# Rounded halves for seven of the last product's projections in a six-product graph kernel

## The chip, the cores and the metric

One core of a Trainium2 chip runs the kernel. The metric is the device time of one execution in microseconds (us), as a median over runs. Engines are named as in the profile: PE is TensorE's matmul, PEld its load of stationary values, DVE is VectorE, ACT is ScalarE, POOL is GpSimd, SP is SyncE.

## The reference, cut to what matters

Everything is fp32. `adj` is a sparse 4096x4096 matrix stored densely, `x` is 4096x128.

```python
def mlp(x, W1, b1, W2, b2, W3, b3):        # leaky_relu with slope 0.01 after each
    x = a(x @ W1 + b1); x = a(x @ W2 + b2)
    return a(x @ W3 + b3)

u = x
for _ in range(3):                          # the third u is not used
    v = mlp(adj @ u, uv_W1, ..., uv_b3)
    u = mlp(adj @ v, vu_W1, ..., vu_b3)
x = layernorm(x + v)                        # products 0 to 4 of the kernel
x = layernorm(x + adj @ (x @ weight))       # product 5: computed as (adj @ x) @ weight
```

## The kernel before, in words

There are six products `adj @ p`, five with the layers of an `mlp` behind them (the fifth with a layer norm too), and a last one, product 5, with one projection by `gcn_W` and a layer norm. The matrix is read as tiles of 256 columns by 512 rows of `adj` (128 x 1024 fp32 in SBUF). Each product has eight output chunks of 512 rows, and each chunk is a sum over 16 tiles in one PSUM bank of 512 columns.

**Halves.** A factor of a product is not used as fp32. ACT rounds it to fp32r (`high`, `p_high`, `h_high`) and DVE subtracts that from the value (`low`, `p_low`, `h_low`), and PE then adds three passes: low by high, high by high, high by low. For the matrix this is done for each tile: SP loads it into one of eight `raw` places, two tiles at a time, ACT writes `high` (L446), DVE writes `low` (L570), both in rings of eight slots. For the stationary side it is done once for each chunk of the vector `p`; `p_high[i]` and `p_low[i]` are 128x4096 each, with i the parity of the product, so product 5 reads the set 1 and product 4 the set 0.

**Order.** All engines walk over the same list of steps. Step n of PE is visit n: one tile times its two stationary blocks, six matmuls of 512 columns (`multiply`, L790). There are 768 visits of 500 tiles, since some tiles serve two products while they are in SBUF. The last product begins in step 594 and is alone from step 686 on. ACT rounds a tile up to 6 steps (`AHEAD`) before PE first visits it, DVE subtracts 4 steps before. Each engine's queue is in order, so whatever is put into step n on an engine stands ahead of the tile work of that step.

**The work of a chunk of the last product** (`not layered(i)`, chunks 40 to 47 of 48) is placed relative to its `start`, the step in which its sum is complete. The starts are 710, 713, 722, 725, 736, 739, 752 and 768.
- start: DVE adds the sum in PSUM and the part kept in SBUF into `h[i % 2]` (`finish`, L604, total_ready). For the last chunk ACT copies the sum instead (`take`).
- start + 4 (`PROJECT`): PE projects, `project` with `turning`: four blocks of `h` are the stationary side, `gcn_W` moves with 128 columns, both fp32, into the one bank `proj`. It waits until the chunk before has been added (x_added), as that empties `proj`.
- start + 5: DVE `measure`: adds the residual (L640), takes statistics (L644, L647). It waits for normed_ready of the chunk before.
- start + 6 and + 7: ACT `deviation` (L504); DVE `invert` (L654, L656, `shift`).
- start + 8: ACT `normalize`, four instructions (L513), and a store from POOL, for the last two chunks from SP.

The layers of the other products run with halves too where `chunk.halves` is set (`dense`, L708 to L711), all but the third, which is an fp32 projection by `turning`.

Of the kernel before, what the change touches and what calls it, by code (L numbers as in the profile page):

```python
# [12 lines left out]
D = 128  # L13
# [34 lines left out]

THIRD, P_LOWER = 1, 2
MEASURE, ROOT, INVERT, NORMALIZE, NORM_P_LOWER = 2, 3, 4, 5, 6  # L50

PROJECT, LAST_MEASURE, LAST_ROOT, LAST_INVERT, LAST_NORMALIZE = 4, 5, 6, 7, 8

# [193 lines left out]
def gnn_kernel(nc, adj, x_nodes, weights, biases, spread, out):  # L247
# [4 lines left out]
    with ExitStack() as ctx:  # L252
# [6 lines left out]
        def sem(name):  # L259
            return ctx.enter_context(nc.semaphore(name))  # L260
# [41 lines left out]
        sum_raised = sem("sum_raised")  # L302
        sum_lowered = sem("sum_lowered")
        taken = sem("taken")
        layer_1_done = sem("layer_1_done")
        first_raised = sem("first_raised")
        first_ready = sem("first_ready")
# [58 lines left out]

        def layered(i):
            return i < FINAL

        def plain(i):  # L370
            return i < NORM
# [69 lines left out]
        def _(act):  # L441
# [75 lines left out]
            def raise_normed(i):  # L517
                c = sum_of(i).chunk
                act.wait_ge(normed_ready, i - NORM + 1)
                act.wait_ge(visited, over_with(LAST - 2, c))  # L520
                nc.scalar.activation(p_high[LAST % 2][:, blocks_of(c)], resid[:, blocks_of(c)],
                                     ACT.Copy).then_inc(p_high_ready, 1)

            def take(i):
                wait_sum(i)
                if plain(i - 2):
                    act.wait_ge(p_low_ready, CHUNKS + i - 1)
                nc.scalar.activation(h[i % 2][:], acc[sum_of(i).bank][:], ACT.Copy).then_inc(taken, 1)

            for n in range(END):  # L530
                if n == TILES - 1:
                    raise_weights()
                for i, chunk in enumerate(chunks):
                    if n == chunk.start and not chunk.halves and not finishes(i):
                        take(i)
                    if layered(i):
                        if n == chunk.start and chunk.halves:
                            raise_sum(i)
                        if n == chunk.start + (LAYER_1 if chunk.halves else WHOLE_LAYER_1):
                            first_layer(i)  # L540
                        if n == chunk.start + (LAYER_2 if chunk.halves else WHOLE_LAYER_2):
                            second_layer(i)
                        if n == chunk.third + THIRD:
                            third_layer(i)
                    if normed(i):
                        if n == chunk.third + ROOT:
                            deviation(i)
                        if n == chunk.third + NORMALIZE:
                            normalize(i)
                            raise_normed(i)  # L550
                    if not layered(i):
                        if n == chunk.start + LAST_ROOT:
                            deviation(i)
                        if n == chunk.start + LAST_NORMALIZE:
                            normalize(i)
                for s in sums:
                    if s.goal == "keep" and n == s.read:
                        keep(s)
                for t in range(len(tiles)):
                    if n == split_at[t]:  # L560
                        if t % IN_BAND == 0 and t // IN_BAND < CHUNKS:
                            raise_x(t // IN_BAND)
                        split(t)
# [3 lines left out]
        def _(dve):  # L567
# [91 lines left out]
            def lower_normed(i):  # L659
                c = sum_of(i).chunk  # L660
                dve.wait_ge(p_high_ready, CHUNKS + i + 1)
                nc.vector.tensor_tensor(p_low[LAST % 2][:, blocks_of(c)], resid[:, blocks_of(c)],
                                        p_high[LAST % 2][:, blocks_of(c)].bitcast(F32),
                                        ALU.subtract).then_inc(p_low_ready, 1)

            for n in range(END):
                if n == TILES - 1:
                    lower_weights()
                for i, chunk in enumerate(chunks):
                    if n == chunk.start and finishes(i):  # L670
                        finish(i)
                    if layered(i):
                        if n == chunk.start + LOWER_SUM and chunk.halves:
                            lower_sum(i)
                        if n == chunk.start + LOWER_FIRST and chunk.halves:
                            lower_first(i)
                        if n == chunk.third:
                            add_bias(i)
                    if plain(i) and n == chunk.third + P_LOWER:
                        lower_third(i)  # L680
                    if normed(i):
                        if n == chunk.third + MEASURE:
                            measure(i)
                        if n == chunk.third + INVERT:
                            invert(i)
                        if n == chunk.third + NORM_P_LOWER:
                            lower_normed(i)
                    if not layered(i):
                        if n == chunk.start + LAST_MEASURE:
                            measure(i)  # L690
                        if n == chunk.start + LAST_INVERT:
                            invert(i)
                for s in sums:
                    if s.goal == "more" and n == s.read:
                        grow(s)
                for t in range(len(tiles)):
                    if n == lowered_at[t]:
                        if t % IN_BAND == 0 and t // IN_BAND < CHUNKS:
                            lower_x(t // IN_BAND)
                        split(t)  # L700
# [3 lines left out]
        def _(pe):  # L704
# [8 lines left out]
            def wait_sum(i):  # L713
                if finishes(i):
                    pe.wait_ge(total_ready, sum_of(i).nth + 1)
                else:
                    pe.wait_ge(taken, unsummed(i) + 1)
# [25 lines left out]
            def turning(i, source, weight):  # L743

                for j in range(IN_CHUNK):
                    done = nc.tensor.matmul(block_in(proj, j), block_in(source, j), weight[:], start=True,  # L746
                                            stop=True)
                done.then_inc(proj_done, 1)
# [5 lines left out]
                turning(i, h[i % 2], w[f"{way_of(i)}_W3"])  # L754

            def project(i):
                wait_sum(i)
                if i > FINAL:
                    pe.wait_ge(x_added, i - NORM)
                else:  # L760
                    pe.wait_ge(biased, FINAL)
                turning(i, h[i % 2], w["gcn_W"])

            def wait_bank(before):
# [76 lines left out]
```

## Time and profile before

| | |
|---|---|
| time, median of 3 runs | 1181.62 us (1181.33 to 1182.02) |
| the profiled execution | 1181.15 us, of which the profile's span is 1179.2 us |
| PE busy | 1154.8 us, 98% |
| DVE busy | 739.8 us, 63% |
| ACT busy | 680.8 us, 58% |
| mean granted clock of PE | 0.999 of full speed |
| last product alone | from about 1048 us to the end |

A start in a timeline is in us from the beginning of the span. The recorded duration of a matmul contains its latency: neighbouring starts tell its cost. An instruction of DVE or ACT can start a little before the end of the one ahead of it. Idle time in brackets names what released the instruction. One fp32 matmul leaves two records of a load and a matmul, one of fp32r leaves one.

### The profile page before, as it was taken

The page shows a single profiled execution, that of the slowest core. Times are in us where ns is not written, and L with a number is a line of the kernel's source. Part 1 is how long each engine was busy: PE and PEld are TensorE (multiplying, and loading weights), DVE is VectorE, ACT ScalarE, POOL GpSimd, SP SyncE. Part 2 cuts the span into 40 slices and gives each one's busy share as a digit, 9 for nine tenths or more (in the row PEclk, how much of TensorE's full clock was granted, in tenths as well). Part 3 has the DMA queues.
Part 4 walks back from the last instruction along what each step waited for, and adds up shares of the span by engine and source line. Part 5 has one row for each costly group of instructions (what it writes and reads, how often), then busy time and mean ns, then how long its engine had stood idle before and what let it go on. Part 6 is the DMA issues. An engine that isn't in the chain of part 4 may idle for free.

```text
span 1179.2 us, 13786 instructions
## 1 busy us (share of the span) xinstructions
PE 1154.8 (98%) x5216; PEld 950.7 (81%) x5216; DVE 739.8 (63%) x879; ACT 680.8 (58%) x855; POOL 10.5 (1%) x24
## 2 busy tenths in 40 slices
PE   5999999999999999999999999999999999999997
PEld 3788888888788888888888878888887888888886
DVE  5986555554845554765564484555578655669996
ACT  5876544555554444764454474544477655557784
POOL 2000000000000000000000000000000000000000
PEclk9999999999999999999999999999999999999999
DMA  8987665644834446645544574444657454458994
GB/s 351 382 317 276 230 248 214 250 160 189 306 148 186 178 185 219 261 169 193 214 183 162 209 289 176 178 178 178 250 215 266 162 185 181 185 195 342 353 347 173
DMA packets 37823, 267.82 MB, mean 227 GB/s; under 512 B 4464, under 2 KB 4464, under 8 KB 5632
## 3 DMA queue, kind: packets, MB, share of 16 engines
q1 hardware_dynamic: 36864, 264.78, 60.0%
q0 software_dynamic: 896, 2.17, 0.5%
q8 instruction: 43, 0.70, 0.2%
q14 instruction: 20, 0.16, 0.0%
HBM read 264.83 MB, written 2.10 MB: 226 GB/s over the span
## 4 chain that ended last, share of the span: by engine, by line
PE 91%; DVE 5%; DMA 3%; ACT 1%; issue 1%; ACTq 0%; SPq 0%; DVEq 0%
PE acc L790 82%; PE proj L746 3%; DVE low L570 3%; DMA raw<-adj_dram 3%; PE layer L711 1%; PE layer L708 1%; PE layer L709 1%; PE layer L740 1%; PE layer L729 1%; DVE stats L644 0%; ACT part L513 0%; DVE h L640 0%; ACT high L446 0%; DVE h L604 0%; DVE moments L647 0%
## 5 line engine op out<-in xcount | busy, mean ns | idle before, releaser
L790 PE MATMUL acc<-high,p_low 128*128 128x512 f32 x1536 | 609.3, 397 | 14.2 <-DVE low L570 14.2
L570 DVE TENSOR_TENSOR low<-raw,high 128x1024 fp32r<-128x1024 f32 x500 | 584.5, 1218 | 36.8 <-ACT high L446 36.8
L790 PE MATMUL acc<-low,p_high 128*128 128x512 f32 x1536 | 599.6, 390 | 0.0
L790 PE MATMUL acc<-high,p_high 128*128 128x512 f32 x1536 | 598.9, 390 | 0.0
L446 ACT ACTIVATE high<-raw 128x1024 fp32r<-128x1024 f32 x500 | 500.2, 1050 | 80.9 <-DMA raw<-adj_dram 40.8
L790 PEld LDWEIGHTS acc<-high,p_low 128*128 128x128 f32 x1536 | 289.1, 188 | 78.9 <-DVE low L570 17.8
L790 PEld LDWEIGHTS acc<-high,p_high 128*128 128x128 f32 x1536 | 289.1, 188 | 61.4 <-issue 2.9
L790 PEld LDWEIGHTS acc<-low,p_high 128*128 128x128 f32 x1536 | 288.9, 188 | 61.4
L473 ACT ACTIVATE h_high<-h 128x512 fp32r<-128x512 f32 x21 | 13.3, 632 | 134.1 <-DVE h L604 134.1
L604 DVE TENSOR_TENSOR h<-acc,part 128x512 f32<-128x512 f32 x36 | 24.8, 689 | 100.8 <-PE acc L790 93.2
L614 DVE TENSOR_TENSOR h_low<-h,h_high 128x512 fp32r<-128x512 f32 x32 | 22.1, 692 | 70.2 <-ACT h L483 70.2
L619 DVE TENSOR_TENSOR h<-proj,b_uv_b 128x512 f32<-128x512 f32 x24 | 16.6, 690 | 63.9 <-PE proj L746 63.9
L609 DVE TENSOR_TENSOR h_low<-acc,h_high 128x512 fp32r<-128x512 f32 x11 | 7.6, 691 | 77.8 <-ACT h_high L473 77.8
L498 ACT ACTIVATE p_high<-h 128x512 fp32r<-128x512 f32 x32 | 20.2, 632 | 48.5 <-DVE h L619 48.0
L473 ACT ACTIVATE h_high<-acc 128x512 fp32r<-128x512 f32 x11 | 6.6, 596 | 72.1 <-PE acc L790 72.1
L619 DVE TENSOR_TENSOR h<-proj,b_vu_b 128x512 f32<-128x512 f32 x16 | 11.1, 691 | 41.6 <-PE proj L746 41.6
L488 ACT ACTIVATE h<-layer,b_uv_b 128x512 f32<-128x512 f32 x24 | 16.5, 688 | 30.3 <-PE layer L711 24.3
L481 ACT ACTIVATE h_high<-layer,b_uv_b 128x512 fp32r<-128x512 f32 x20 | 13.7, 686 | 34.1 <-PE layer L711 34.1
L500 ACT ACTIVATE h<-h 128x512 f32<-128x512 f32 x40 | 24.8, 620 | 9.9 <-DVE h L619 9.8
L746 PEld LDWEIGHTS proj<-w_uv_W,h 128*128 128x128 f32 x192 | 25.1, 191 | 2.0
L463 ACT ACTIVATE part<-acc 128x512 f32<-128x512 f32 x36 | 21.4, 595 | 7.4 <-PE acc L790 7.0
L746 PE MATMUL proj<-w_uv_W,h 128*128 128x128 f32 x192 | 25.3, 275 | 0.0
(64 smaller groups left out, 379.6 us busy)
## 6 DMA issues: line engine op xcount, KB each, us to landing
raw<-adj_dram SPq DMA_DIRECT2D x250, 1024.0 KB, 4.9
out_dram<-part POOLq DMA_DIRECT2D x6, 256.0 KB, 5.1
resid<-x_dram SPq DMA_DIRECT2D x1, 1024.0 KB, 18.2
resid<-x_dram SPq DMA_DIRECT2D x2, 256.0 KB, 5.9
resid<-x_dram SPq DMA_DIRECT2D x1, 512.0 KB, 13.0
out_dram<-part SPq DMA_DIRECT2D x2, 256.0 KB, 2.0
w_uv_W<-uv_W_dram POOLq DMA_DIRECT2D x3, 64.0 KB, 7.8
w_vu_W<-vu_W_dram POOLq DMA_DIRECT2D x3, 64.0 KB, 7.9
```

What stands on the lines that cost most here:

```text
L446: nc.scalar.activation(high[t % SLOTS][:], raw_of(t), ACT.Copy).then_inc(high_ready, 1)
L463: nc.scalar.activation(part_of(s.chunk), acc[s.bank][:], ACT.Copy).then_inc(part_kept, 1)
L473: nc.scalar.activation(h_high[:], summed(i)[:], ACT.Copy).then_inc(sum_raised, 1)
L488: nc.scalar.activation(h[i % 2][:], layer[1][:], ACT.Prelu, bias=b[f"{way_of(i)}_b2"][:], alpha=SLOPE).then_inc(second_ready, 1)
L498: nc.scalar.activation(p_high[k % 2][:, blocks_of(c)], h[i % 2][:], ACT.Prelu, alpha=SLOPE).then_inc(p_high_ready, 1)
L500: nc.scalar.activation(h[i % 2][:], h[i % 2][:], ACT.Prelu, alpha=SLOPE).then_inc(third_ready, 1)
L570: nc.vector.tensor_tensor(low[t % SLOTS][:], raw_of(t), high[t % SLOTS][:].bitcast(F32), ALU.subtract).then_inc(low_ready, 1)
L604: nc.vector.tensor_tensor(h[i % 2][:], acc[s.bank][:], part_of(s.chunk), ALU.add).then_inc(total_ready, 1)
L614: nc.vector.tensor_tensor(h_low[:], h[i % 2][:], h_high[:].bitcast(F32), ALU.subtract).then_inc(first_lowered, 1)
L619: nc.vector.tensor_tensor(h[i % 2][:].rearrange("p (j d) -> p j d", d=D), proj[:].rearrange("p (j d) -> p j d", d=D), b_spread[f"{way_of(i ...
L746: done = nc.tensor.matmul(block_in(proj, j), block_in(source, j), weight[:], start=True, stop=True)
L790: done = nc.tensor.matmul(bank[:], p[parity][:, at:at + D], a[slot][:, columns], start=(n == s.opens and j == 0 and m == 0), stop=(n == s. ...
```

## The change

Seven of the eight chunks of the last product (`projects_halves(i)`: chunks 40 to 46) are projected in three passes of rounded halves. The room for them is the stationary set 0, which product 4 no longer reads from step 686 on: `spare_of(i)` are the first seven blocks of 512 columns of `p_high[0]` and `p_low[0]`, and `SPARE_W` the first 128 columns of the eighth, for `gcn_W`. Added are:
- once: ACT rounds `gcn_W` in step 707 (`raise_gcn`), DVE subtracts in step 708 (`lower_gcn`), 128x128 each.
- for each of the seven chunks: ACT rounds `h` (128x512) in step start, ahead of the other work of that step (`raise_last`); it waits for total_ready. DVE subtracts in step start + 1 (`lower_last`).
- on PE, in place of four fp32 matmuls (128x128 by 128x128): twelve fp32r matmuls of the same shape, behind waits for `last_lowered` and `gcn_lowered` in place of total_ready.

Chunk 47 is projected as before. Nothing changes in the order of the visits, the loads from HBM or the buffers of the tiles.

```diff
--- before.py
+++ after.py
@@ -48,6 +48,7 @@
 
 THIRD, P_LOWER = 1, 2
 MEASURE, ROOT, INVERT, NORMALIZE, NORM_P_LOWER = 2, 3, 4, 5, 6
+
 
 PROJECT, LAST_MEASURE, LAST_ROOT, LAST_INVERT, LAST_NORMALIZE = 4, 5, 6, 7, 8
 
@@ -302,6 +303,10 @@
         sum_raised = sem("sum_raised")
         sum_lowered = sem("sum_lowered")
         taken = sem("taken")
+        gcn_raised = sem("gcn_raised")
+        gcn_lowered = sem("gcn_lowered")
+        last_raised = sem("last_raised")
+        last_lowered = sem("last_lowered")
         layer_1_done = sem("layer_1_done")
         first_raised = sem("first_raised")
         first_ready = sem("first_ready")
@@ -367,6 +372,16 @@
         def layered(i):
             return i < FINAL
 
+        def projects_halves(i):
+            return FINAL <= i < len(chunks) - 1
+
+        def spare_of(i):
+            return blocks_of(i - FINAL)
+
+        SPARE_W = bass.ds((CHUNKS - 1) * CHUNK, D)
+
+        FREED = 1 + max(n for n, v in enumerate(visits) if sums[v.total].product == NORMED)
+
         def plain(i):
             return i < NORM
 
@@ -520,6 +535,15 @@
                 act.wait_ge(visited, over_with(LAST - 2, c))
                 nc.scalar.activation(p_high[LAST % 2][:, blocks_of(c)], resid[:, blocks_of(c)],
                                      ACT.Copy).then_inc(p_high_ready, 1)
+
+            def raise_gcn():
+                act.wait_ge(visited, FREED)
+                nc.scalar.activation(p_high[0][:, SPARE_W], w["gcn_W"][:], ACT.Copy).then_inc(gcn_raised, 1)
+
+            def raise_last(i):
+                wait_sum(i)
+                act.wait_ge(visited, FREED)
+                nc.scalar.activation(p_high[0][:, spare_of(i)], h[i % 2][:], ACT.Copy).then_inc(last_raised, 1)
 
             def take(i):
                 wait_sum(i)
@@ -548,7 +572,11 @@
                         if n == chunk.third + NORMALIZE:
                             normalize(i)
                             raise_normed(i)
+                    if i == FINAL and n == chunk.start - 3:
+                        raise_gcn()
                     if not layered(i):
+                        if n == chunk.start and projects_halves(i):
+                            raise_last(i)
                         if n == chunk.start + LAST_ROOT:
                             deviation(i)
                         if n == chunk.start + LAST_NORMALIZE:
@@ -662,6 +690,16 @@
                 nc.vector.tensor_tensor(p_low[LAST % 2][:, blocks_of(c)], resid[:, blocks_of(c)],
                                         p_high[LAST % 2][:, blocks_of(c)].bitcast(F32),
                                         ALU.subtract).then_inc(p_low_ready, 1)
+
+            def lower_gcn():
+                dve.wait_ge(gcn_raised, 1)
+                nc.vector.tensor_tensor(p_low[0][:, SPARE_W], w["gcn_W"][:], p_high[0][:, SPARE_W].bitcast(F32),
+                                        ALU.subtract).then_inc(gcn_lowered, 1)
+
+            def lower_last(i):
+                dve.wait_ge(last_raised, i - FINAL + 1)
+                nc.vector.tensor_tensor(p_low[0][:, spare_of(i)], h[i % 2][:], p_high[0][:, spare_of(i)].bitcast(F32),
+                                        ALU.subtract).then_inc(last_lowered, 1)
 
             for n in range(END):
                 if n == TILES - 1:
@@ -685,7 +723,11 @@
                             invert(i)
                         if n == chunk.third + NORM_P_LOWER:
                             lower_normed(i)
+                    if i == FINAL and n == chunk.start - 2:
+                        lower_gcn()
                     if not layered(i):
+                        if n == chunk.start + LOWER_SUM and projects_halves(i):
+                            lower_last(i)
                         if n == chunk.start + LAST_MEASURE:
                             measure(i)
                         if n == chunk.start + LAST_INVERT:
@@ -754,11 +796,25 @@
                 turning(i, h[i % 2], w[f"{way_of(i)}_W3"])
 
             def project(i):
-                wait_sum(i)
+                if projects_halves(i):
+                    pe.wait_ge(last_lowered, i - FINAL + 1)
+                else:
+                    wait_sum(i)
                 if i > FINAL:
                     pe.wait_ge(x_added, i - NORM)
                 else:
+                    pe.wait_ge(gcn_lowered, 1)
                     pe.wait_ge(biased, FINAL)
+                if projects_halves(i):
+                    w_high_gcn, w_low_gcn = p_high[0][:, SPARE_W], p_low[0][:, SPARE_W]
+                    s_high, s_low = p_high[0][:, spare_of(i)], p_low[0][:, spare_of(i)]
+                    for j in range(IN_CHUNK):
+                        nc.tensor.matmul(block_in(proj, j), block_in(s_high, j), w_high_gcn, start=True, stop=False)
+                        nc.tensor.matmul(block_in(proj, j), block_in(s_high, j), w_low_gcn, start=False, stop=False)
+                        done = nc.tensor.matmul(block_in(proj, j), block_in(s_low, j), w_high_gcn, start=False,
+                                                stop=True)
+                    done.then_inc(proj_done, 1)
+                    return
                 turning(i, h[i % 2], w["gcn_W"])
 
             def wait_bank(before):
```

## Rows read from the trace of the kernel before

**Rows 1.** The page, part 1: busy us (share of the span) and instructions.
```profile
PE 1154.8 (98%) x5216; PEld 950.7 (81%) x5216; DVE 739.8 (63%) x879; ACT 680.8 (58%) x855; POOL 10.5 (1%) x24
```

**Rows 2.** Busy times of the last stage, 1060 to 1170 us.
```profile
core 0: us, PE busy (x) PEld busy (x) DVE busy (x) ACT busy (x) POOL busy (x), PEclk, DMA share, GB/s
1060.00:1170.00 110.00, 109.11 (x511) 90.44 (x510) 101.42 (x167) 84.06 (x112) 3.25 (x6) 1.00 0.85 329
```

**Rows 3.** Groups by line: busy us, mean ns | idle before.
```profile
L498 ACT ACTIVATE p_high<-h 128x512 fp32r<-128x512 f32 x32 | 20.2, 632 | 48.5 <-DVE h L619 48.0
...
L746 PE MATMUL proj<-w_gcn_W,h 128*128 128x128 f32 x64 | 8.6, 277 | 0.8 <-ACT h L528 0.7
```

**Rows 4.** Waits from 1080 to 1160 us: in total, times, longest.
```profile
PEld acc L790 <- DVE low L570: 1.7, 2, 0.8
```

**Rows 5.** Timeline of DVE: start, duration, count, idle before.
```profile
1072.01 11.44 DVE L570 TENSOR_TENSOR low<-raw,high 128x1024 fp32r<-128x1024 f32 x10
1083.59 0.69 DVE L604 TENSOR_TENSOR h<-acc,part 128x512 f32<-128x512 f32 x1
...
1095.10 0.16 DVE L656 SCALAR_TENSOR_TENSOR shift<-moments,rstd 128x4 f32<-128x4 f32 x1
...
1107.81 0.68 DVE L604 TENSOR_TENSOR h<-acc,part 128x512 f32<-128x512 f32 x1
1108.41 2.35 DVE L570 TENSOR_TENSOR low<-raw,high 128x1024 fp32r<-128x1024 f32 x2
...
1114.91 0.16 DVE L656 SCALAR_TENSOR_TENSOR shift<-moments,rstd 128x4 f32<-128x4 f32 x1
...
1143.46 6.89 DVE L570 TENSOR_TENSOR low<-raw,high 128x1024 fp32r<-128x1024 f32 x6
...
1165.39 2.36 DVE L570 TENSOR_TENSOR low<-raw,high 128x1024 fp32r<-128x1024 f32 x2 [1.04 <-ACT high L446]
```

**Rows 6.** Timeline of PE's matmuls at five places.
```profile
1088.55 0.40 PE L790 MATMUL acc<-low,p_high 128*128 128x512 f32 x1
...
1089.91 0.39 PE L790 MATMUL acc<-high,p_high 128*128 128x512 f32 x1
...
1119.45 0.39 PE L790 MATMUL acc<-low,p_high 128*128 128x512 f32 x1
1120.24 0.50 PE L790 MATMUL acc<-high,p_low 128*128 128x512 f32 x1 [0.40 <-DVE low L570]
1120.58 0.39 PE L790 MATMUL acc<-high,p_high 128*128 128x512 f32 x1
...
1133.32 0.39 PE L790 MATMUL acc<-low,p_high 128*128 128x512 f32 x1
...
1134.97 0.40 PE L790 MATMUL acc<-high,p_high 128*128 128x512 f32 x1
...
1141.37 0.39 PE L790 MATMUL acc<-low,p_high 128*128 128x512 f32 x1
...
1142.51 0.39 PE L790 MATMUL acc<-high,p_high 128*128 128x512 f32 x1
...
1169.08 0.39 PE L790 MATMUL acc<-high,p_low 128*128 128x512 f32 x1
```

**Rows 7.** Timeline of PE's loads at 1142 us.
```profile
1142.17 0.19 PEld L790 LDWEIGHTS acc<-high,p_low 128*128 128x128 f32 x1 [0.84 <-DVE low L570]
1142.28 0.19 PEld L790 LDWEIGHTS acc<-high,p_high 128*128 128x128 f32 x1
```

**Rows 8.** Groups of DVE from 1080 to 1160 us: busy, mean | idle before.
```profile
L570 DVE TENSOR_TENSOR low<-raw,high 128x1024 fp32r<-128x1024 f32 x53 | 61.8, 1215 | 0.3 <-ACT high L446 0.3
...
L640 DVE TENSOR_TENSOR h<-proj,resid 128x512 f32<-128x512 f32 x7 | 4.8, 688 | 2.5 <-ACT part L513 2.5
```

**Rows 9.** Timeline of ACT: two rows of four normalizations each.
```profile
1095.47 1.63 ACT L513 ACTIVATE part<-h,shift,rstd 128x128 f32<-128x128 f32 x4
...
1115.46 1.64 ACT L513 ACTIVATE part<-h,shift,rstd 128x128 f32<-128x128 f32 x4
```

## Prediction

> **What bounds the kernel now.** I read the page first, then the busy times of the last stage, then the waits in it, and last the timelines of DVE, PE and ACT around each place where PE stands still. Over the whole span PE is busy 98% and DVE 63% [rows 1]. But the edit lies in the last product alone, and that stage has another balance: from 1060 to 1170 us PE is busy 109.11 of 110 us, and DVE 101.42 [rows 2]. So there DVE has some 8.6 us left in 110, and PE next to nothing. One must ask for both engines.
>
> The slack between the two can be read visit by visit. PE takes one tile in six passes. Two neighbouring starts are 0.2275 us apart, so a tile costs 1.365 us; DVE makes the low half of one in (6.89 - 0.09)/6 = 1.13 us [rows 5], but once per output chunk it also adds, measures and inverts. DVE starts the stage with a lead over PE; after two pairs of chunks it is used up. At 1120.24 PE waits for DVE's low half, and its load again at 1142.17 [rows 6, 7]: these two are all the waits for `low` that it has there [rows 4]. Their cost comes from the starts: from 1119.45 to 1120.58 are 1.13 us where two undisturbed passes take 0.455, so 0.675 us lost; from 1141.37 to 1142.51 it is 1.14, so 0.685 lost [rows 6]. A third one hides in a projection: from 1133.32 to 1134.97 are 1.65 us, where the same stretch around the first projection (1088.55 to 1089.91) takes 1.36. The 0.29 us more are project(45) waiting for x_added of chunk 44, an addition on DVE. In sum DVE already costs PE 1.65 us, so it is the bound up to 1142 us, and PE is the bound behind it.
>
> **The change on PE.** One projection before is four fp32 products, recorded as eight matmuls (64 for the eight chunks) [rows 3]. It costs 1.36 - 0.455 = 0.905 us of PE [rows 6], 0.113 for each record. After it there are twelve rounded passes with 128 moving columns, each with its own load of stationary values. No row has such a pass, so I bound it:
> - Below: 0.057 us, half a record of 0.113, if the load costs nothing. Twelve are 0.68 us, 0.22 less than before.
> - The load: two loads of rounded halves stand 1142.17 and 1142.28 us, 0.11 apart, when nothing but the load sets the pace [rows 7]. A pass that waits for its load takes at least 0.11. The fp32 records, whose loads run beside the matmul before, keep 0.113; with that twelve are 1.36, or 0.45 us more for each projection.
> - Load and pass one after the other: 0.11 + 0.057 = 0.167; twelve are 2.0, 1.1 more.
> - Above: a pass of 128 columns costs what one of 512 costs, 0.2275; twelve are 2.73, 1.82 more.
>
> I take 0.113, because the passes lie next to the row of back-to-back loads, and because eight fp32 records already run at that pace with their loads behind the pass before. Seven projections: 7 x 0.45 = 3.15 us of PE.
>
> The Trainium skill ("TensorE: Matmul & The Clock Gate", section "Back-to-back issue gap") states that a stream of load and matmul with 128 columns sustains about 81 ns each. By that, as an estimate from the page, twelve would be 0.97 us and a projection would cost 0.07 more, not 0.45; the two loads 0.11 us apart speak against it for this data type, and no row has the pair itself.
>
> **The change on DVE.** lower_last is a subtraction of 128x512. The one like it, L604, starts at 1107.81 and the next instruction at 1108.41, so it takes 0.60 us of the queue [rows 5]. Seven times in the stage: at steps 711, 714, 723, 726, 737, 740 and 753 (one step after a chunk's start, where a step is one visit; PE's stalls are at visits 734 and 748). lower_gcn (128 columns, step 708) is at most 0.6 too; being a quarter as wide I say 0.2, and it falls into the gap in front of the addition at 1083.59 (the ten low halves before it end at 1072.01 + 11.44 = 1083.45, and without a wait the next instruction starts 0.09 before such an end), where the addition waits for PE's sum. Free.
>
> What reaches PE by visit 734: four subtractions, 2.4 us, less what DVE's idle time absorbs. DVE is idle 2.5 us before the addition L640 (three times) and 0.3 before a low half, which waits for ACT [rows 8]. Those 2.5 are no free time: they are the way from `shift` through four normalizations on ACT (1.64 us [rows 9]) to the addition, which waits for normed_ready, with one low half in between; if `shift` comes later, so does all of it. Only where ACT itself was late is there something to gain: L513 starts at 1115.46 while `shift` ended at 1114.91 + 0.16 = 1115.07. With 0.03 for the semaphore 0.36 are absorbed; at 1095.47 against 1095.26 it is 0.18 [rows 5, 9]. The second subtraction falls beside the 0.3 idle, but must wait until ACT has rounded, and gains 0.06. So DVE is 2.4 - 0.6 = 1.8 us later at visit 734. Two more subtractions come before visit 748, with nothing absorbed: 3.0 us.
>
> **On ACT**: raise_last is like L498, 0.63 us [rows 3], seven times, and stands ahead of the next tile's rounding; it waits for total_ready, thus for DVE. ACT works two steps ahead of DVE and is busy only 84.06 of 110 us [rows 2], so I cost it at nothing. Without that cover it is 6 x 0.63 = 3.8 us on DVE's path. Nothing is added to a DMA queue; raw slots come free later only as DVE is later. The waits of project() for last_lowered are met: with DVE as the bound the subtraction (step start + 1) is just done when PE gets to step start + 4.
>
> **The sum.** Up to visit 734 PE has 4 x 0.45 = 1.8 us more work of its own, as much as DVE's delay; up to 748 it has 2.7 against 3.0. PE's additions therefore lie within DVE's delay and the stalls of 1.65 us that are there anyway, and are not added to it. PE comes out of visit 748 3.0 us later. The seventh projection (step 756) is behind it: + 0.45. Its subtraction at step 753 fits into the lead that DVE has by then: the last low half is done at 1165.39 + 2.36 = 1167.75 and PE starts on it at 1169.08 [rows 5, 6], 1.3 us against 0.6. Together + 3.45 us. The profiled execution took 1181.15 us around its span of 1179.2, the median of the runs is 1181.62, which agrees within 0.04%. So 1181.62 + 3.45 = 1185.1 us.
>
> **Rivals.**
> - *DVE's work is hidden* (the other side). If the subtractions fall into the 2.8 us that DVE is idle, only 3.6 - 2.8 = 0.8 us is left, less than PE's own. Then PE decides: 3.15 - 1.65 (its present stalls, filled) = 1.5 us, 1183.1, not to be told from before. For it: the idle time is in the rows. Against: it ends with ACT, whose work starts after DVE's. It decides as soon as DVE's delay at visit 748 falls under 1 us.
> - *Load and pass in series*: 7 x 1.1 - 1.65 = 6.05 us, 1187.7, PE being the bound. Against it: fp32 records overlap theirs.
> - *A short pass costs as a long one*: 7 x 1.82 - 1.65 = 11.1 us, 1192.7. Nothing in the profile excludes it, since each rounded pass there has 512 columns.
> - *Loads hide, passes run at 0.057*: DVE stays the bound, 3.0 - 0.22 = 2.8 us, 1184.4. The row of two loads is against it. The 81 ns of the Trainium skill ("TensorE: Matmul & The Clock Gate", as above) would lie within this case: by an estimate from that page 3.0 + 0.07 = 3.1 us and 1184.7.
> - *ACT's order*: the wait for total_ready at the head of ACT's queue makes the tiles' rounding late, and DVE waits for it: 3.45 + 3.8 = 7.2 us, 1188.8.
>
> **Chances.** The forecast 0.46, hidden 0.15, short as long 0.15, in series 0.12, hidden loads 0.06, ACT's order 0.06. The range takes in all but the 1192.7 (0.15): 1183.0 to 1188.9. The forecast's own is 1184.4 to 1186.0 (0 to 0.8 us absorbed, ends of the rows' rounding). A measurement of this kernel can tell some 0.2%, 2.4 us, so the limit is 1184.0. Slower: all but the hidden case and a third of the hidden loads, 0.81; same 0.17; faster 0.02, since no mechanism that I see takes DVE's work away.
>
> **What would show it.** The new passes' loads 0.11 us apart, a projection at 1.35 us of PE; PE's waits for `low` at visits 734 and 748 still there, and DVE without idle time but for the normalization's. The low half before visit 748 some 3 us later in the span than 1142.1. Wrong would be: twelve passes over 1.5 us or under 1.1; PE's waits for DVE gone (then PE decides); new waits of DVE for `high` (ACT's order).

## The result, and the profile after

Over ten runs each, the changed kernel takes 1184.42 us in the median (1183.57 to 1185.05) and the kernel before 1181.38 (1180.15 to 1185.7). The ratio is 1.0021, with a 95% interval of 1.0013 to 1.0029: 2.5 us slower by the ratio, 3.0 by the medians. The forecast was 1185.1 and slower.

The first 850 us of two executions differ by up to 2 us (visit 560 starts at 854.8 to 856.8 us in all but one of the traces below, and at 858.4 us in kernel 11). A stretch inside the last product is therefore the sharper measure: from the last pass of visit 713, just before the first projection, to the first pass of the last visit, 767. Before it is 1169.08 - 1088.55 = 80.53 us [rows 6]. I call it the stage and give it for every kernel; it is read from one execution each, and a late load or a chain of waits can lengthen it in a single execution by more than a microsecond, as kernels 3 and 8 show below; so differences of a few tenths count only where the places they come from are read as well. After the change the stage is 1172.78 - 1088.66 = 84.12 us, 3.6 more.

Busy times of the same stretch as [rows 2], after:

```profile
1060.00:1170.00 110.00, 109.09 (x523) 90.43 (x522) 104.45 (x174) 88.54 (x120) 3.24 (x6) 1.00 0.87 329
```

PE is as full as before; DVE went from 101.42 to 104.45 us and ACT from 84.06 to 88.54.

PE's matmuls at the places of [rows 6], after (the first projection, visit 734, the sixth projection, visit 748, the last visit), and the fourth projection, which comes second here:

```profile
1088.66 0.39 PE L846 MATMUL acc<-low,p_high 128*128 128x512 f32 x1
1088.88 0.22 PE L812 MATMUL proj<-p_high 128*128 128x128 f32 x1
1088.94 0.28 PE L813 MATMUL proj<-p_low,p_high 128*128 128x128 f32 x1
1089.05 0.27 PE L814 MATMUL proj<-p_high,p_low 128*128 128x128 f32 x1
...
1090.46 0.40 PE L846 MATMUL acc<-high,p_high 128*128 128x512 f32 x1
...
1113.26 0.39 PE L846 MATMUL acc<-low,p_high 128*128 128x512 f32 x1
1113.86 0.30 PE L812 MATMUL proj<-p_high 128*128 128x128 f32 x1 [0.22 <-DVE h L668]
...
1115.52 0.40 PE L846 MATMUL acc<-high,p_high 128*128 128x512 f32 x1
...
1121.91 0.39 PE L846 MATMUL acc<-low,p_high 128*128 128x512 f32 x1
1122.26 0.50 PE L846 MATMUL acc<-high,p_low 128*128 128x512 f32 x1
1122.60 0.39 PE L846 MATMUL acc<-high,p_high 128*128 128x512 f32 x1
...
1135.91 0.39 PE L846 MATMUL acc<-low,p_high 128*128 128x512 f32 x1
1136.99 0.30 PE L812 MATMUL proj<-p_high 128*128 128x128 f32 x1 [0.70 <-DVE h L668]
...
1138.65 0.40 PE L846 MATMUL acc<-high,p_high 128*128 128x512 f32 x1
...
1145.04 0.39 PE L846 MATMUL acc<-low,p_high 128*128 128x512 f32 x1
1145.39 0.50 PE L846 MATMUL acc<-high,p_low 128*128 128x512 f32 x1
1145.73 0.39 PE L846 MATMUL acc<-high,p_high 128*128 128x512 f32 x1
...
1172.78 0.39 PE L846 MATMUL acc<-high,p_low 128*128 128x512 f32 x1
```

The passes start 0.11 us apart. The projection takes 1090.46 - 1088.66 - 0.455 = 1.345 us, against 0.905: 0.44 more, 0.112 a pass. The matrix passes right behind it also start up to 0.01 us further apart than usual, and more of them do so than before; counted to the twelfth pass behind, a projection costs 0.47 more, 3.3 us for seven. This is the 0.47 of the expectations below. PE still stands still at visits 734 and 748, but for 0.69 - 0.455 = 0.235 us each, not 0.68. The sixth projection has become the larger stop: 1138.65 - 1135.91 = 2.74 us, of which 0.455 + 1.345 are work, so 0.94 are lost, where it was 0.29. The fourth projection stops PE too, as it did not before: 1115.52 - 1113.26 = 2.26 us, so 0.46 are lost, and the fifth loses 0.10 (1130.34 to 1132.24) on `p_low`. In sum PE now loses 0.46 + 0.235 + 0.10 + 0.94 + 0.235 = 1.97 us to DVE, where it was 1.65. With the 3.3 us of its own that makes 3.3 + 1.97 - 1.65 = 3.6, the measured difference. The waits say what for; from 1080 to 1160 us, as [rows 4]:

```profile
ACT p_high L546 <- DVE h L632: 4.2, 6, 1.1
DVE h L668 <- ACT part L528: 2.3, 3, 1.0
...
PE proj L812 <- DVE h L668: 0.9, 2, 0.7
PEld acc L846 <- DVE low L598: 0.8, 2, 0.4
PEld proj L812 <- DVE p_low L701: 0.2, 1, 0.2
```

PE waits for `h L668`, the addition whose x_added lets the next projection into `proj`. DVE, as [rows 5]:

```profile
1081.21 0.29 DVE L696 TENSOR_TENSOR p_low<-w_gcn_W,p_high 128x128 fp32r<-128x128 f32 x1
...
1083.70 0.69 DVE L632 TENSOR_TENSOR h<-acc,part 128x512 f32<-128x512 f32 x1
...
1085.44 0.68 DVE L701 TENSOR_TENSOR p_low<-h,p_high 128x512 fp32r<-128x512 f32 x1
1086.04 2.35 DVE L598 TENSOR_TENSOR low<-raw,high 128x1024 fp32r<-128x1024 f32 x2
...
1098.35 0.69 DVE L668 TENSOR_TENSOR h<-proj,resid 128x512 f32<-128x512 f32 x1 [1.03 <-ACT part L528]
...
1119.22 0.69 DVE L668 TENSOR_TENSOR h<-proj,resid 128x512 f32<-128x512 f32 x1 [0.65 <-ACT part L528]
```

`L701` at 1085.44 is a subtraction of the change: 0.60 us to the next start. `L696` at 1081.21 (gcn_W, 0.20 to the next start at 1081.41) costs nothing: the addition behind it, at 1083.59 before, is at 1083.70 with the whole trace 0.11 later.

### The profile page after: what moved, and what is told of

Read it like the earlier page. It is cut to its first block, busy times and chain, and to the rows that moved or that the text cites. A ratio compares the mean times of both kernels' runs of the same rounds, so it can differ in the third digit from the quotient of the medians.

```text
span 1183.0 us, 13865 instructions
## 1 busy us (share of the span) xinstructions
PE 1157.5 (98%) x5244; PEld 953.1 (81%) x5244; DVE 744.1 (63%) x887; ACT 685.4 (58%) x863; POOL 10.5 (1%) x24
## 4 chain that ended last, share of the span: by engine, by line
PE 90%; DVE 6%; DMA 3%; ACT 1%; issue 1%; ACTq 0%; SPq 0%; DVEq 0%
PE acc L846 81%; DVE low L598 4%; PE proj L788 3%; DMA raw<-adj_dram 3%; PE layer L753 1%; PE layer L750 1%; PE layer L751 1%; PE layer L782 1%; PE layer L771 1%; DVE stats L672 0%; DVE h L668 0%; ACT part L528 0%; DVE h L632 0%; DVE p_low L701 0%; ACT high L461 0%
## 5 line engine op out<-in xcount | busy, mean ns | idle before, releaser
L647 DVE TENSOR_TENSOR h<-proj,b_uv_b 128x512 f32<-128x512 f32 x24 | 16.6, 690 | 63.9 <-PE proj L788 63.9
L647 DVE TENSOR_TENSOR h<-proj,b_vu_b 128x512 f32<-128x512 f32 x16 | 11.1, 691 | 41.6 <-PE proj L788 41.6
```

The lines of the kernel that those rows point to most:

```text
L647: nc.vector.tensor_tensor(h[i % 2][:].rearrange("p (j d) -> p j d", d=D), proj[:].rearrange("p (j d) -> p j d", d=D), b_spread[f"{way_of(i ...
```

## The experiments

Each kernel is compared with the kernel before on the same chip. The diffs are cut to their core. Kernels 1, 3, 4, 8 and 11 leave work or operands out, so their output is not that of the reference; they are there for their time alone.

| kernel | ratio to before, 95% interval | median, before | stage (before 80.53) |
|---|---|---|---|
| the change | 1.0021 (1.0013 to 1.0029) | 1184.42, 1181.38 | +3.6 |
| 1 passes only | 1.0006 (0.9997 to 1.0015) | 1182.27, 1181.43 | +1.7 |
| 2 halves only | 1.0022 (1.0013 to 1.0032) | 1183.71, 1181.43 | +3.2 |
| 3 before, short statistics | 0.9982 (0.9973 to 0.9991) | 1179.12, 1181.43 | see there |
| 4 after, short statistics | 1.0014 (1.0005 to 1.0022) | 1182.66, 1181.43 | +2.2 |
| 5 before, LAG 1 | 0.9984 (0.9975 to 0.9994) | 1180.82, 1182.04 | -1.0 |
| 6 after, LAG 1 | 1.0020 (1.0010 to 1.0031) | 1184.10, 1182.04 | +4.2 |
| 7 GpSimd subtracts | 1.0066 (1.0042 to 1.0090) | 1190.61, 1182.04 | +12.4 |
| 8 64 columns | one run | 1185.67, 1182.04 | +5.1 |
| 9 before, LAG 1, two banks | 0.9984 (0.9973 to 0.9996) | 1180.05, 1181.43 | -1.0 |
| 10 after, LAG 1, two banks | 1.0026 (1.0015 to 1.0036) | 1185.06, 1181.43 | +4.2 |
| 11 passes only, LAG 1, two banks | 1.0006 (0.9997 to 1.0016) | 1182.72, 1181.43 | +1.6 |
| 12 after, two banks | 1.0019 (1.0010 to 1.0028) | 1183.71, 1181.43 | +3.2 |

**1. Passes only.** PE does the twelve passes, nobody makes halves.

```diff
-                    if i == FINAL and n == chunk.start - 3:
-                        raise_gcn()
...
-                        if n == chunk.start and projects_halves(i):
-                            raise_last(i)
...
-                    if i == FINAL and n == chunk.start - 2:
-                        lower_gcn()
...
-                        if n == chunk.start + LOWER_SUM and projects_halves(i):
-                            lower_last(i)
...
             def project(i):
-                if projects_halves(i):
-                    pe.wait_ge(last_lowered, i - FINAL + 1)
-                else:
-                    wait_sum(i)
+                wait_sum(i)
...
-                    pe.wait_ge(gcn_lowered, 1)
```

> The seven projections run in twelve rounded passes, but nothing makes their halves: raise_last, lower_last and the two for gcn_W are left out, and the passes read what product 4 left in the set 0 (the output is that of other operands). PE waits for the sum as before. Theory of the prediction (VectorE is the bound up to visit 748): PE's extra 7 x 0.47 = 3.3 us fill its present waits of 1.65 us first, so + 1.6 us against the kernel before, and no wait for low at visits 734 and 748. Rival (the passes alone cost the time): + 3.0 to 3.3 us, as the whole change.

Measured: 1.7 us more in the stage, 0.8 by the medians. PE has no wait for `low` and none for x_added between 1080 and 1160 us; all that it loses is its own work, which filled the old waits first. The passes alone do not explain 3.6.

**2. Halves only.** All work on ACT and DVE, fp32 on PE.

```diff
-                if projects_halves(i):
-                    w_high_gcn, w_low_gcn = ...
...
-                    done.then_inc(proj_done, 1)
-                    return
                 turning(i, h[i % 2], w["gcn_W"])
```

> ScalarE and VectorE make all halves as in the changed kernel and PE waits for them, but projects in four fp32 matmuls of h and gcn_W as before. Theory of the prediction: VectorE sets the time up to visit 748, so + 3.2 us against the kernel before, all but the last projection's 0.47 of the whole change, with longer waits of PE for low at visits 734 and 748. Rival (the subtractions are hidden in VectorE's idle time): within 0.5 us of the kernel before.

Measured: 3.2 us more in the stage, as expected, 2.3 by the medians. So the subtractions are not hidden, and nearly the whole cost is there without a single new pass. The waits of this kernel, 1080 to 1160 us:

```profile
PE proj L788 <- DVE h L668: 2.3, 2, 1.2
...
PEld acc L836 <- DVE low L598: 1.7, 2, 0.9
...
PEld proj L788 <- DVE p_low L701: 1.0, 2, 0.7
PE acc L836 <- DVE low L598: 0.9, 2, 0.4
```

PE, with less of its own to do than in the changed kernel, waits longer for each of the three things that DVE makes: `low`, x_added, `p_low`. The two parts, 1.7 and 3.2 us, would make 4.9 if they added up; the change costs 3.6. The runs alone cannot show this: by the ratios the parts cost 0.7 and 2.6 us and the change 2.5, each within about 1 us. The traces show it: up to visit 748 kernel 2 is 3.2 us later than the kernel before (1145.05 - 1087.86 against 1142.51 - 1088.55) and the changed kernel 3.1, although it has the passes too.

**3 and 4. Short statistics**, in the kernel before and after.

```diff
-                    nc.vector.bn_stats(stats[:, j, :], block_in(h[i % 2], j)).then_inc(stats_ready, 1)
+                    nc.vector.bn_stats(stats[:, j, :], (block_in(h[i % 2], j) if layered(i)
+                                       else h[i % 2][:, j * D:j * D + 16])).then_inc(stats_ready, 1)
```

> The kernel before, with the statistics of the last product taken over 16 of 128 columns (other means and variances; all instructions and waits stay). That takes some 0.1 us off each of four instructions, about 0.45 us of VectorE for each chunk, 2.7 us before visit 748. Theory (VectorE is the bound there already, PE loses 1.65 us to it): - 1.3 to - 1.65 us, and PE's waits for low at visits 734 and 748 gone. Rival (PE is the bound, its waits are noise): within 0.4 us of the kernel before.

> The changed kernel with the same short statistics. Theory (VectorE's queue is what the change lengthens, and PE stands behind it): VectorE's delay at visit 748 falls from 3.2 to some 0.5 us, so PE decides and the time is that of the passes alone, + 1.6 us against the kernel before, half of the change. Rival (only the passes cost): + 3.0 us or more, as without the edit.

The kernel before gets 2.1 us faster by the ratio (2.3 by the medians), more than I expected. I had left out the last chunk, whose statistics stand at the end with nothing beside them. There the four instructions take 0.32 us where they took 0.79 (the start of `L647` less that of `L644`: 1175.85 - 1175.53 against 1173.99 - 1173.20):

```profile
1173.20 0.87 DVE L644 BATCH_NORM_STATS2 stats<-h 128x6 f32<-128x128 f32 x4
1173.99 0.36 DVE L647 BATCH_NORM_AGGREGATE moments<-stats 128x2 f32<-128x6 f32 x4
```

```profile
1175.53 0.41 DVE L644 BATCH_NORM_STATS2 stats<-h 128x6 f32<-128x16 f32 x4
1175.85 0.37 DVE L647 BATCH_NORM_AGGREGATE moments<-stats 128x2 f32<-128x6 f32 x4
```

1.65 + 0.47 = 2.1. (The profiled execution of kernel 3, 1183.18 us, had ACT wait 4.1 us for one load and is far above its median, so its stage is not given. In that trace PE still waits behind the late load, so whether its old waits are gone cannot be read there.) The agreement with 1.65 + 0.47 is closer than the runs can tell, whose interval is 1.1 us either way. In the changed kernel the same relief leaves 1.65 us over the kernel before by the ratio and 1.2 by the medians; without the 0.47 won at the end that makes 2.1 or 1.7, and the stage says 2.2, against 1.6 expected. In its trace PE has no wait for `low`; 0.4 us for x_added is left. Work taken from VectorE's queue comes back as time, in both kernels, so that queue was the bound.

**5 and 6. LAG 1.** DVE makes each low half one step earlier.

```diff
-LAG = 2
+LAG = 1
```

> The kernel before with LAG 1 in place of 2: VectorE makes each low half one step earlier (5 steps ahead of its visit, not 4), so it stands ahead of one more step of measuring and subtracting. No work is added or removed. Theory (PE loses 1.65 us to VectorE's lead being used up at visits 734 and 748): one more tile of lead, 1.1 to 1.4 us at each, removes both waits: - 1.4 us, at most - 1.65. Rival (ScalarE's rounding, now one step ahead of VectorE and fed by the loads, holds VectorE up instead): 0 or slower, with waits of low for high.

> The changed kernel with LAG 1. Theory: the same extra lead takes 1.1 to 1.4 us off VectorE's delay of 3.2 at visit 748, which leaves 1.9 to 2.1; PE's own bound is 1.65: + 1.9 to + 2.6 us against the kernel before (the last projection's 0.47 is behind it). Rival: as in the run beside it, no gain, + 3 us or more.

The kernel before becomes faster by 0.16% (0.06 to 0.25%), with no work removed: PE's waits for `low` are gone from the stage. But only 1.0 us of the gain is there, since the sixth projection now loses 2.09 - 1.36 = 0.73 us (1132.68 to 1134.77) where it lost 0.29; another 1.1 us are won at visit 595, in the fifth product, at the first layer of a chunk, where PE's wait for `h_high` falls from 1.41 to 0.35 us (from start to start 0.74 us where it was 1.80). What DVE or ACT does earlier for it I have not followed. In the kernel before and in this one:

```profile
910.78 0.39 PE L790 MATMUL acc<-low,p_high 128*128 128x512 f32 x1
912.58 0.47 PE L708 MATMUL layer<-h_high,w_low_uv_W 128*128 128x512 f32 x1 [1.41 <-ACT h_high L473]
```

```profile
911.95 0.39 PE L790 MATMUL acc<-low,p_high 128*128 128x512 f32 x1
912.69 0.47 PE L708 MATMUL layer<-h_high,w_low_uv_W 128*128 128x512 f32 x1 [0.35 <-ACT h_high L473]
```

For the changed kernel the total (2.1 us over before) falls into what I expected, and yet the reason was wrong. The stage became longer, 4.2 against 3.6 us, and the total is helped by those 1.1 us at visit 595, which its trace has too. (4.2 - 1.1 = 3.1 is still more than the 2.1 to 2.4 of the runs.) With LAG 1 one more low half stands ahead of lower_last in DVE's queue, and now the projection waits for that:

```profile
1128.64 0.39 PE L846 MATMUL acc<-low,p_high 128*128 128x512 f32 x1
1129.66 0.33 PE L812 MATMUL proj<-p_high 128*128 128x128 f32 x1 [0.64 <-DVE p_low L701]
```

The extra lead went to the tiles and was taken from the projections.

**7. GpSimd subtracts.** lower_last goes from DVE's list of steps to POOL's, with each store at its place.

```diff
-                        if n == chunk.start + LOWER_SUM and projects_halves(i):
-                            lower_last(i)
...
+            for n in range(END):
+                for i in range(FINAL, len(chunks) - 1):
+                    if n == chunks[i].start + LOWER_SUM:
+                        lower_last(i)
+                    if n == chunks[i].start + LAST_NORMALIZE and i < len(chunks) - 2:
+                        store(i)
```

> The changed kernel with the seven subtractions of h (lower_last) on GpSimd, in its order between the stores, and all else as it is. Theory (it is the place in VectorE's queue that costs, not the work or the later PE waits): the passes' cost is left, + 1.6 us against the kernel before. Rival (GpSimd is too slow, so that PE waits for last_lowered, or VectorE's instructions beside it get longer): + 3 us or more.

The rival holds: 7.8 us slower by the ratio. The six runs fall into two groups, 1187.5 to 1188.1 and 1193.1 to 1194.6 us, and the profiled one, with 12.4 us more in the stage, is of the second. POOL takes 1.54 us for what DVE does in 0.60, and once 4.91, and PE waits 3.32 us for that one; and DVE's work beside it gets longer:

```profile
1084.49 1.54 POOL L449 TENSOR_TENSOR p_low<-h,p_high 128x512 fp32r<-128x512 f32 x1 [1076.19 <-ACT p_high L558]
...
1156.90 4.91 POOL L449 TENSOR_TENSOR p_low<-h,p_high 128x512 fp32r<-128x512 f32 x1 [5.64 <-ACT p_high L558]
```

```profile
1083.65 4.59 DVE L610 TENSOR_TENSOR low<-raw,high 128x1024 fp32r<-128x1024 f32 x3
...
1156.06 6.83 DVE L610 TENSOR_TENSOR low<-raw,high 128x1024 fp32r<-128x1024 f32 x5
```

Three low halves take 4.59 us, where 3 x 1.13 + 0.09 = 3.5 are usual [rows 5]: 1.1 us lost on DVE. Five take 6.83 beside the long one, where 5 x 1.13 + 0.09 = 5.74 are usual: again 1.1. So DVE loses 1.1 us for each subtraction on POOL, more than the 0.60 that it saves.

Part of the 12.4 us is another thing. PE's granted clock falls to half twice in this execution, from about 1116.3 to 1119.7 and from about 1160.7 to 1167.5 us (columns as in [rows 2], the clock third from the end):

```profile
1116.00:1118.00 2.00, 2.00 (x9) 1.62 (x8) 2.00 (x2) 2.00 (x3) 0.00 (x0) 0.58 0.22 90
...
1164.00:1166.00 2.00, 2.00 (x8) 1.71 (x8) 1.24 (x4) 0.98 (x2) 0.00 (x0) 0.50 0.97 410
```

There PE's 512-column passes start 0.43 us apart and the new passes 0.21, against 0.2275 and 0.112. From start to start the two stretches are about 4 us longer than the same work at full clock, an estimate from those starts, so some 8 of the 12.4 us are left for the waits and the passes. The first fall came 1.5 us after a wait of 1.16 us for x_added, the second during the wait of 3.32; a wait of 1.18 us in kernel 2 had no fall behind it, so what sets it off these traces do not show. The clock is not the whole cost: the one run whose mean clock is 0.999 took 1188.1 us.

**8. 64 columns.** Each pass moves half of gcn_W.

```diff
-                        nc.tensor.matmul(block_in(proj, j), block_in(s_high, j), w_high_gcn, start=True, stop=False)
...
+                        half = block_in(proj, j)[:, :64]
+                        nc.tensor.matmul(half, block_in(s_high, j), w_high_gcn[:, :64], start=True, stop=False)
...
```

> The changed kernel with each of the passes moving 64 of gcn_W's 128 columns, into half of each block (the other half keeps old sums). If the load of 128 stationary columns sets the pace of a pass, as the prediction takes it, the starts stay 0.11 us apart and a projection costs 1.36 us as before. If the moving columns do, the starts come closer, down to half.

```profile
1088.86 0.28 PE L813 MATMUL proj<-p_high 128*128 128x64 f32 x1
1088.97 0.28 PE L814 MATMUL proj<-p_low,p_high 128*128 128x64 f32 x1
```

Half the columns, the same 0.11 us between starts, and a projection takes the same 1.345 us. So the moving columns do not set the pace. That the load does follows with the two loads 0.11 us apart [rows 7]; no run changed the stationary side. (This execution's stage is longer than that of the changed kernel by 1.5 us through waits of DVE and PE elsewhere; with one run I make nothing of it.)

**9 to 12. Two banks.** Every second projection goes into layer 0's bank.

```diff
+        def bank_of(i):
+            return proj if i < FINAL or (i - FINAL) % 2 == 0 else layer[0]
...
             def project(i):
...
-                if i > FINAL:
-                    pe.wait_ge(x_added, i - NORM)
+                if i > FINAL + 1:
+                    pe.wait_ge(x_added, i - NORM - 1)
+                elif i == FINAL + 1:
+                    pe.wait_ge(first_ready, FINAL)
```

> The kernel before with LAG 1, and every second projection of the last product goes into layer 0's bank, which is free by then, so that project no longer waits for x_added of the chunk before. No work is added or removed. Theory: LAG 1 alone left a wait of 0.72 us there (visit 743); without it all of PE's 1.65 us of waits in the last product are gone, and some 1.2 us between visits 560 and 600 with LAG 1: - 2.5 to - 2.9 us against the kernel before. Rival (something else holds PE there): - 1.9 us, as with LAG 1 alone.

> The changed kernel with LAG 1 and the two banks. With LAG 1 the projections waited for last_lowered and for x_added; the second is gone here. Theory (PE waits for lower_last, which is behind one more tile now): between PE's own bound of 3.3 us over the run beside it and 3.6: + 0.6 to + 1.2 us against the kernel before. Rival (x_added was all that held it): exactly 3.3 over the run beside it and no wait for p_low.

> As the first of these three, with the seven projections in twelve passes over what is left in the set 0 and no work on ScalarE or VectorE for it (the output is that of other operands). With no wait of PE left to fill, the passes' whole price must show: 7 x 0.47 = 3.3 us over the first of the three, + 0.5 us against the kernel before. If it is below 2 us, the price of a pass was read wrongly.

> The changed kernel (LAG 2) with the two banks alone. Theory (VectorE's low half at visit 748 sets the time, and the wait of the sixth projection for x_added ahead of it only takes its place): the time of the changed kernel, + 3.0 us against the kernel before, with longer waits for low in place of those for x_added. Rival (the wait for x_added is a cost of its own): 1.4 to 2.0 us less than the changed kernel.

Kernel 12 went as expected: without the wait for x_added the sixth projection no longer stops PE, and the time stays within what the runs can tell (1.0019 against 1.0021), since the wait for `low` at visit 748 takes its place:

```profile
1144.47 0.39 PE L853 MATMUL acc<-low,p_high 128*128 128x512 f32 x1
1145.75 0.50 PE L853 MATMUL acc<-high,p_low 128*128 128x512 f32 x1 [0.89 <-DVE low L601]
```

From 1144.47 to 1145.75 are 1.28 us, 1.05 more than a pass, where the changed kernel had 0.35 from start to start. Kernel 9 fell short of the 2.5 to 2.9 us expected: 1.9 us faster by the ratio and 1.4 by the medians, no better than LAG 1 alone (the rival). PE's waits between 1080 and 1160 us are down to one stop for `low` again, at visit 748 (1140.27 to 1141.40, 0.68 us lost). DVE's own waits for `high` (1.7 us, behind the loads) may be a part of it; that is not shown:

```profile
ACT high L449 <- DMA raw<-adj_dram: 11.7, 12, 1.7
...
DVE low L573 <- ACT high L449: 1.7, 5, 0.4
PEld acc L796 <- DVE low L573: 1.0, 2, 0.8
PE acc L796 <- DVE low L573: 0.4, 1, 0.4
```

Kernel 10 is slower than kernel 9 by 5.0 us in the medians, more than the 3.3 to 3.6 that I gave it, and slower than the kernel before by 3.6 (3.1 by the ratio), not by 0.6 to 1.2; in the stage it is 5.1 over kernel 9. With x_added out of the way the projection waits for `p_low` alone, 2.1 us in two waits, one of 1.00 at the fifth projection and one of 1.09 at the seventh:

```profile
1155.37 0.33 PE L819 MATMUL proj<-p_high 128*128 128x128 f32 x1 [1.09 <-DVE p_low L704]
```

```profile
PE proj L819 <- DVE p_low L704: 2.1, 2, 1.1
```

Kernel 11 has the passes without halves and no wait of PE in the stage: 1.6 us longer than before, about 3.3 - 1.65. Against kernel 9, which has 0.68 us of waits left to fill, it is 2.5 us in the stage, where 3.3 - 0.68 = 2.6 would come out if the passes fill that wait first. By the medians it is 2.7, less than my 3.3 and more than the 2 under which the price of a pass would have been wrong.

## Why the prediction was right

The time lies in the range, but the range took in all rivals but one. The runs alone say little between them: the ratio's interval is 1.5 to 3.4 us slower, with "hidden" (1.5) at its lower end and the forecast (3.45) at its upper one, and "loads hide" (2.8) inside. What tells them apart is the traces, step by step.

- *What bounds.* That PE loses 1.65 us to DVE before the change, at visits 734, 743 and 748, stands in the starts, and two runs bear it out: short statistics give 2.1 back (0.47 of it at the end), and LAG 1 removes the two waits for `low`.
- *A pass at 0.113 us, paced by the load of the stationary side.* 0.112 in the trace after; kernel 8, with half the columns, shows the same. With the slower passes behind it a projection costs 0.47 us, not 0.45. The 81 ns that the Trainium skill ("TensorE: Matmul & The Clock Gate", section "Back-to-back issue gap") gives for 128 columns is not reached by fp32r operands in these traces. The rivals "in series" and "short as long" are out by the same rows.
- *A subtraction at 0.60 us, gcn_W's free.* Both as read above.
- *What DVE's idle time absorbs.* At visit 734 DVE is 2.02 us later by the raw traces, less the 0.11 by which the whole trace is later: 1.9, forecast 1.8. At visit 748 it is 3.22 - 0.11 = 3.1 (the pass behind PE's stop starts at 1145.73 against 1142.51), forecast 3.0. The parts were less exact than the sum, which came out near by luck. The wait for normalization at 1119.22 is 0.65 us where it was 0.99, the 0.36 that I had read from ACT's lateness; but the one at 1098.35 grew from 0.81 to 1.03, since ACT was now late there, and the second subtraction moved the low half behind it from 1089.71 only to 1090.65, so that 0.4 of it fell into DVE's wait for `high`, where I gave it 0.06.
- *DVE's work is not hidden.* That rival asked for 1.5 us and no waits for DVE; kernel 2 has 3.2 us from DVE's and ACT's part alone.
- *PE's additions lie within DVE's delay, but for the last.* Kernel 2 has the stage at + 3.2 without them, the change at + 3.6; the 0.4 between them is the seventh projection: behind visit 748 kernel 2 takes 26.56 us to the last visit, the kernel before 26.57 and the change 27.05. The sum was 3.45, the stage says 3.6, the runs 2.5 (ratio) and 3.0 (medians).
- *Waits of project().* Here one step was incomplete. I had the wait for x_added in the stalls before, but let it stay small; it grew from 0.29 to 0.94 us, a new one of 0.46 came at the fourth projection, and the waits for `low` shrank from 0.68 to 0.24 each. That the subtraction would be "just done" when PE comes for it held but for 0.10 us at the fifth projection. The end is nearly the same, since all of them wait for the same queue, and kernel 12 shows that the one takes the other's place.
- *ACT's order.* ACT waits 4.2 us for total_ready in all, six times; DVE never waits for `p_high`. Hidden, as forecast. (In kernel 2 DVE waits for `p_high` once, 0.4 us.)

## What to carry to other kernels

Read the cost of a new matmul from the load as well as from the columns: in these traces an fp32r pass that moves 128 columns against 128 stationary ones costs what its load costs, so three such passes (3 x 0.112 = 0.34 us) are dearer than the fp32 matmul that they replace (0.905 / 4 = 0.23). Where one engine waits for another that is itself almost full, add up each engine's new work to the point where they last meet, take the larger, and add what comes behind it; the parts do not add. And a wait that disappears from a trace proves nothing by itself: with LAG 1 and with two banks it came back under another name, at the same producer.

The kernel before with LAG 1 beats both: 0.9984 (0.9975 to 0.9994) of the kernel before, with one constant changed. Two banks on top of it give nothing that these runs can tell.

## What the runs showed of the hardware

GpSimd and VectorE hold each other up on fp32 subtractions from SBUF: 128x512 took GpSimd 1.54 us and once 4.91 (VectorE takes 0.60), and VectorE lost 1.1 us of its own low halves beside each, the long one too, as the rows of kernel 7 show. The Trainium skill ("SBUF — State Buffer", section "SBUF: two separate sides") states that a VectorE operation with two SBUF inputs and a GpSimd operation that reads SBUF take one pair of ports in turn, each for its whole instruction. The trace agrees with turns being taken, though the runs do not show the ports.
